# Cross-attention of a Perceiver layer: turning the probabilities by VectorE blocks and a DMA exchange in place of TensorE transposes

## The reference, cut to what matters

```python
x = x + xattn(layernorm(x), ctx, mask, Wq, Wk, Wv, Wo)      # ctx: 32 x 512 x 384
x = x + attn(layernorm(x), wq, wk, wv, wo)
x = x + ffn(layernorm(x), router, W1, b1, W2, b2)
def xattn(x, ctx, mask, ...):                                # 16 heads of 32
    scores = einsum('bhid,bhjd->bhij', q, k) * scale         # 64 queries x 512 keys for each head
    attn = softmax(where(mask, scores, -max), axis=-1)
    return (einsum('bhij,bhjd->bhid', attn, v)).reshape(...) @ Wo
```

## Time and profile before

| what | value |
|---|---|
| median of 3 launches | 1335.34 us (1334.23 to 1335.86) |
| span of the profiled execution | 1332.7 us |
| PE busy | 1313.8 us, 99% of the span |
| DVE, ACT, POOL busy | 52%, 53%, 44% of the span |
| matmul instructions | 13380 |
| mean DMA rate | 50 GB/s |

### The profile page before, as it was taken

How to read it: one execution, slowest core, us unless ns; L and a number is a source line. 1 busy time by engine, 2 the same in 40 slices (tenths; PEclk the granted TensorE clock), 3 DMA queues, 4 the chain that set the end, 5 groups by cost and what they waited for, 6 DMA issues and landing times.

```text
span 1332.7 us, 33915 instructions
## 1 busy us (share of the span) xinstructions
PE 1313.8 (99%) x13380; PEld 1057.2 (79%) x13380; DVE 691.3 (52%) x1693; ACT 710.4 (53%) x1380; POOL 585.8 (44%) x316
## 2 busy tenths in 40 slices
PE   7999999999999999999999999999999998999998
PEld 6877777777777777777777777788998997888786
DVE  4244544545444445545444454456666669755623
ACT  6455656666566656566565666674332345634231
POOL 6722522332243234224323422576666565473562
PEclk9999999999999999999999999999999999999999
DMA  7101010111111111110101113010000001323241
GB/s 262 60 27 35 28 59 26 33 42 42 33 33 51 33 33 42 42 33 26 59 26 33 34 51 128 15 58 2 2 3 3 1 18 49 96 95 96 80 141 63
DMA packets 39316, 66.46 MB, mean 50 GB/s; under 512 B 4177, under 2 KB 8529, under 8 KB 39249
## 3 DMA queue, kind: packets, MB, share of 16 engines
q1 hardware_dynamic: 38816, 64.70, 14.9%
q10 hardware_dynamic: 432, 0.79, 0.2%
HBM read 61.28 MB, written 4.19 MB: 49 GB/s over the span
## 4 chain that ended last, share of the span: by engine, by line
PE 95%; DVE 3%; issue 1%; DMA 1%; SPq 0%; ACT 0%; POOL 0%; POOLq 0%; DVEq 0%
PE psum L205 41%; PE psum L253 8%; PE psum L2031 7%; PE psum L1678 7%; PE psum L1021 6%; PE psum L223 5%; PE psum L241 5%; PE psum L262 3%; PE psum L1010 3%; PE psum L1041 3%; PE psum L777 2%; PE psum L1052 1%; PE psum L1060 1%; PE psum L1070 1%; DMA tok<-in_x 1%
## 5 line engine op out<-in xcount | busy, mean ns | idle before, releaser
L303 ACT ACTIVATE PT<-psum 128x512 f32<-128x512 f32 x256 | 153.2, 598 | 227.1 <-PE psum L253 227.1
L290 ACT ACTIVATE prob<-prob,nmx 128x512 f32<-128x512 f32 x256 | 182.5, 714 | 96.4 <-DVE nmx L351 96.4
L365 DVE COPY V<-psum 128x512 f32<-128x512 f32 x128 | 88.5, 692 | 228.1 <-PE psum L205 228.1
L351 DVE CUSTOM_DVE_ANT_0 prob<-psum,mbias 128x512 f32<-128x512 f32 x256 | 165.4, 684 | 66.1 <-PE psum L223 66.1
L498 POOL TENSOR_SCALAR ctx_a<-ctx_r 128x1536 fp32r<-128x1536 f32 x16 | 65.4, 4088 | 279.2 <-PE psum L205 279.0
L296 ACT ACTIVATE prob<-prob,rinv 128x512 f32<-128x512 f32 x256 | 182.5, 713 | 0.0
L498 POOL TENSOR_SCALAR ctx_b<-ctx_r 128x1536 fp32r<-128x1536 f32 x16 | 65.4, 4088 | 235.5 <-PE psum L205 235.5
L253 PEld LDWEIGHTS psum<-ident,prob 128*128 128x128 f32 x1024 | 127.5, 141 | 32.8
L253 PE MATMUL psum<-ident,prob 128*128 128x128 f32 x1024 | 153.1, 272 | 0.0
L205 PE MATMUL psum<-wv_h,ctx_b 128*128 128x512 f32 x384 | 144.4, 417 | 0.0
L205 PE MATMUL psum<-wv_h,ctx_a 128*128 128x512 f32 x384 | 142.1, 412 | 0.0
(11 more groups left out here) (238 smaller groups left out, 2934.4 us busy)
## 6 DMA issues: line engine op xcount, KB each, us to landing
ctx_r<-in_ctx SPq DMA_DIRECT2D x32, 768.0 KB, 4.6
w_r<-in_L_ffn_W SPq DMA_DIRECT2D x64, 256.0 KB, 2.9
xres<-in_x SPq DMA_DIRECT2D x16, 256.0 KB, 2.6
out<-tok SPq DMA_DIRECT2D x13, 256.0 KB, 3.4
tok<-in_x SPq DMA_DIRECT2D x3, 1024.0 KB, 11.9
mask<-in_mask_BxS_bf SPq DMA_DIRECT2D x32, 64.0 KB, 4.2
tok<-in_x SPq DMA_DIRECT2D x4, 256.0 KB, 3.5
wq_r<-in_L_xattn_Wq SPq DMA_DIRECT2D x4, 256.0 KB, 5.0
```

What stands on the lines that cost most here:

```text
L290: act.activation(prob[:, r, :], prob[:, r, :], ACT.Exp, bias=nmx[:, r:r + 1], scale=-1.0, accum_out=rsum[:, r:r + 1]).then_inc(s_ex, 1)
L303: act.activation(PT[:, r, :, :].rearrange("p k n -> p (k n)"), T_bank, ACT.Copy).then_inc(s_Pt, 1)
L351: dve.tensor_tensor_reduce(prob[:, r, :], S_bank[r], mbias[:, b, :], 1.0, 3.0e38, ALU.add, ALU.min, nmx[:, r:r + 1]).then_inc(s_mx, 1)
L365: dve.tensor_copy(item_place(q, m), KV_bank[m % 2]).then_inc(s_KVe, 1)
```

## The change

In tiles 0 to 14 (60 groups) TensorE no longer transposes probabilities and ScalarE no longer copies `PT`. VectorE turns each scaled slot in 32x32 blocks into `blocks` (`dve_blocks`, one instruction of 128x512 for each slot), which leaves each block in its own 32 partitions. SyncE then exchanges the 4 x 4 grid of 32-partition parts with 16 DMAs of 64 KB each from `blocks` to `turned` (`sp_exchange`). `blocks` and `turned` have two buffers by the parity of q. The value products of a group read `turned` two groups later instead of one. The output product moves from q = 0 to q = 1, between items 1 and 2, into the bank that the transposes used; the residual addition moves to the end of VectorE's list at q = 1, the statistics to the end at q = 2. VectorE still copies all four items; the semaphore of those copies is split in two. Tile 15 keeps the transposes (`pe_last_group` and so on); its q = 0 does the value products of two earlier groups, and the loads of the self-attention weights wait for the last exchange. An unused function `dve_slot` goes.

```diff
+        blocks = [m(f"blocks{i}", [P, 4, 4, KT, HD], F32) for i in range(2)]
+        turned = [Map(nc, pt_at)("turned0", [P, 4, 4, KT, HD], F32), m("turned1", [P, 4, 4, KT, HD], F32)]
...
+        def pe_exchanged_values(pe, g, q, first=False):
+            i, z = GPT * g + q, (q - 2) % GPT
+            pe.wait_ge(s_ex4[z], 256 * (g + 1 if q >= 2 else g))
+            if not (first and q == 2):
+                pe.wait_ge(s_Ol, i - 2)
+            value_products(pe, z, lambda c, kt, r: turned[z % 2][:, 2 * c:2 * c + 2, r, kt, :], PV_bank)
...
-        def pe_group(pe, g, q, first=False, fill=None, filled=None):
+        def pe_group(pe, g, q, first=False):
             pe_scores(pe, g, q, first)
-            if not (first and q == 0):
-                pe_values(pe, g, q, first)
+            if not (first and q < 2):
+                pe_exchanged_values(pe, g, q, first)
+            pe_item(pe, g, q, 0)
+            pe_item(pe, g, q, 1)
+            if q == 1 and not first:
+                pe_outputs(pe, g, T_bank)
+            pe_item(pe, g, q, 2)
+            pe_item(pe, g, q, 3)
...
+        def act_group(act, g, q, first=False):
             act_exp(act, g, q, 0)
             act_exp(act, g, q, 1)
+            if not (first and q < 2):
+                act_outputs(act, g, q, 2, first)
+            act_norm(act, g, q, 0)
+            act_exp(act, g, q, 2)
+            act_norm(act, g, q, 1)
+            act_exp(act, g, q, 3)
+            act_norm(act, g, q, 2)
+            act_norm(act, g, q, 3)
...
+        def dve_blocks(dve, g, q, r, first=False):
+            i = GPT * g + q
+            dve.wait_ge(s_pn, 4 * i + r + 1)
+            if r == 0 and not (first and q < 2):
+                dve.wait_ge(s_PV, i - 1)
+            dve.transpose(blocks[q % 2][:, :, r, :, :].rearrange("p g k n -> p k g n"),
+                          prob[:, r, :].rearrange("p (k g n) -> p k g n", g=4, n=HD)).then_inc(s_bl, 1)
...
+        def dve_group(dve, g, q, first=False):
+            dve_max(dve, g, q, 0, first)
             dve_max(dve, g, q, 1)
             dve_max(dve, g, q, 2)
             dve_inverse(dve, g, q, 0)
             dve_max(dve, g, q, 3)
             dve_inverse(dve, g, q, 1)
+            if not (first and q < 2):
+                dve_outputs(dve, g, q, 2)
+            dve_blocks(dve, g, q, 0, first)
+            dve_item(dve, g, q, 0)
+            dve_inverse(dve, g, q, 2)
+            dve_blocks(dve, g, q, 1)
+            dve_inverse(dve, g, q, 3)
+            dve_item(dve, g, q, 1)
+            dve_blocks(dve, g, q, 2)
+            dve_blocks(dve, g, q, 3)
+            dve_item(dve, g, q, 2)
+            dve_item(dve, g, q, 3)
+            if q == 1 and not first:
+                dve_add(dve, g, T_bank)
+            if q == 2 and not first:
+                dve_stats(dve, g)
...
+        def sp_exchange(sp, g, q, first):
+            i = GPT * g + q
+            sp.wait_ge(s_bl, 4 * i + 4)
+            settle(sp)
+            if not (first and q < 2):
+                sp.wait_ge(s_PV, i - 1)
+            settle(sp)
+            for e in range(4):
+                for f in range(4):
+                    sp.dma_start(turned[q % 2][f * HD:(f + 1) * HD, e].rearrange("p r k n -> p (r k n)"),
+                                 blocks[q % 2][e * HD:(e + 1) * HD, f].rearrange("p r k n -> p (r k n)"))\
+                        .then_inc(s_ex4[q], 16)
...
         def sp_tile(sp, g, first, last):
             if last:
+                sp.wait_ge(s_ex4[3], 256 * (G - 1))
                 for i, r, w in ((1, kw_r, ak), (0, qw_r, aq), (2, vw_r, av)):
                     sp.dma_start(r[:], w.rearrange("(t p) n -> p t n", p=P)).then_inc(s3_w[i], 16)
+                sp_tokens(sp, g, first)
+                return
+            sp_context(sp, g, 2, False)
+            sp_exchange(sp, g, 0, first)
+            sp_exchange(sp, g, 1, first)
+            sp_context(sp, g, 3, False)
+            sp_exchange(sp, g, 2, first)
+            sp_tokens(sp, g, first)
+            sp_exchange(sp, g, 3, first)
...
             pool.wait_ge(s3_w[1], 16)
+            pool.wait_ge(s_PV, OWN)
             pool_split(pool, kw_h, kw_l, kw_r)
```

More of the change, by code:

```diff
@@ L196, in pe_item @@
                     pe.wait_ge(s_cx, 2 * (BPG * g + q // HALVES + 2))
-                if not (isinstance(i, int) and i < 0 and m < 2):
-                    pe.wait_ge(s_KVe, 4 * i + 3 + m)
+                if m >= 2:
+                    pe.wait_ge(s_Ke, 2 * i + 1 + m)
+                elif not (isinstance(i, int) and i < 0):
+                    pe.wait_ge(s_Ve, 2 * i + 1 + m)
             for c in parts:
@@ L208, in pe_item, with pe_scores @@
                 ins.then_inc(s_KV, 1)
-        def pe_scores(pe, g, q, first):
+        def pe_scores(pe, g, q, first, last=False):
             i, b, a = GPT * g + q, q // HALVES, q % HALVES
@@ L214, in pe_scores @@
                 pe.wait_ge(s_qb, BPG * g + b + 1)
-            pe.wait_ge(s_KVe, 4 * i + 2)
+            pe.wait_ge(s_Ke, 2 * i + 2)
             if not (first and q == 0):
                 pe.wait_ge(s_mx, 4 * i)
-            if q == 1 and not first:
+            if q == 1 and last:
                 pe.wait_ge(s_x1, g + 1)
@@ L225, in pe_scores, with value_products @@
             ins.then_inc(s_S, 1)
-        def pe_values(pe, g, q, first, place=PV_bank):
-            i, z = GPT * g + q, (q - 1) % GPT
+        def value_products(pe, z, source, place):
             b, a = z // HALVES, z % HALVES
[L232 to L236, removed]
             for c in range(2):
@@ L258, in pe_outputs @@
             pe.wait_ge(s_Ol, GPT * g)
-            pe.wait_ge(s_mx, 4 * GPT * g + 1 if place is Wo_bank else 4 * GPT * g)
+            if place is Wo_bank:
+                pe.wait_ge(s_mx, 4 * GPT * g + 1)
+            elif place is T_bank:
+                pe.wait_ge(s_x1, g)
+            else:
+                pe.wait_ge(s_mx, 4 * GPT * g)
             for n in range(DT):
@@ L273, in pe_group @@
             pe_item(pe, g, q, 1)
+            if q == 0:
+                pe_exchanged_values(pe, g, 1)
             if filled:
                 pe.wait_ge(*filled)
-            pe_turn(pe, g, q, 0, first)
-            if q == 0 and not first:
-                pe_outputs(pe, g)
+            pe_turn(pe, g, q, 0)
             pe_item(pe, g, q, 2, (0, 1))
             pe_turn(pe, g, q, 1)
+            if q == 0:
+                pe_outputs(pe, g)
             pe_item(pe, g, q, 2, (2,))
@@ L334, in act_group @@
                 act_exp(act, g, q, 3)
-                act_turn(act, g, q, 0, first)
+                act_turn(act, g, q, 0)
             act_norm(act, g, q, 2)
@@ L342, in act_group, with dve_max @@
             act_turn(act, g, q, 3)
-        def dve_max(dve, g, q, r):
+        def dve_max(dve, g, q, r, first=False, last=False):
             i, b = GPT * g + q, q // HALVES
@@ L347, in dve_max @@
                 dve.wait_ge(s_S, i + 1)
+                if not (first and q == 0) and not (last and q > 0):
+                    dve.wait_ge(s_bl, 4 * i)
                 if q % HALVES == 0:
@@ L380, in dve_group, with dve_last_group @@
             dve_inverse(dve, g, q, 1)
-            if not (first and q == 0):
-                dve_outputs(dve, g, q)
+            if not (first and q < 2):
[14 more added lines that the diff above has]
+                dve_stats(dve, g)
+        def dve_last_group(dve, g, q, fill=None):
+            dve_max(dve, g, q, 0, last=True)
+            dve_max(dve, g, q, 1)
+            dve_max(dve, g, q, 2)
+            dve_inverse(dve, g, q, 0)
+            dve_max(dve, g, q, 3)
+            dve_inverse(dve, g, q, 1)
+            dve_outputs(dve, g, q, 2 if q == 0 else 1)
             dve_item(dve, g, q, 0)
@@ L388, in dve_group @@
             dve_inverse(dve, g, q, 3)
-            if q == 0 and not first:
+            if q == 0:
+                dve_outputs(dve, g, 1, 2)
+            dve_item(dve, g, q, 2)
+            if q == 0:
                 dve_add(dve, g)
-            dve_item(dve, g, q, 2)
-            if q == 1 and not first:
+            if q == 1:
                 dve_stats(dve, g)
@@ L420, in layer_norm @@
                            bias=sh3[:, bass.ds(t, 1)], scale=rs3[:, bass.ds(t, 1)]).then_inc(s3_xn, 1)
[L422 to L463, removed]
         def sp_context(sp, g, b, first):
@@ L475, in sp_context, with sp_tokens @@
             sp.dma_start(mask8[:, b % BPG, :], mask[bass.ds(n, 1), :].broadcast_to([P, SK])).then_inc(s_mraw[b % BPG], 16)
[L477 to L482, removed]
+        def sp_exchange(sp, g, q, first):
[10 more added lines that the diff above has]
+                        .then_inc(s_ex4[q], 16)
+        def sp_tokens(sp, g, first):
             if not first:
@@ L486, in sp_tile @@
             sp.dma_start(xres[:], xt[:, bass.ds(g, 1), :]).then_inc(s_xr, 16)
-            if not last:
-                sp_context(sp, g, 3, False)
+        def sp_tile(sp, g, first, last):
```

(25 more changed lines are left out.)

91 lines of the change are left out of this document (56 added, 35 removed).

## The result

The changed kernel takes 1246.45 us (median of 4 launches, 1244.41 to 1247.91) against 1335.17 us before (4 launches); the ratio is 0.9336, 95% interval 0.9323 to 0.9349. That is 88.7 us faster where 104 were forecast. The profiled execution has a span of 1245.9 us, 86.8 less than before. So the direction and most of the size came, and some 15 us did not.

A forecast was written before the change was run, and what follows sets the result against it. TensorE, busy 1313.8 of 1332.7 us, was taken as the bound. Turns 110, less 4 for statistics and 2 for tile 15's stall, gave 104: span 1228.7, plus 2.6 for launches, 1231 us; range 1222 to 1265.

The forecast's parts named there:

- TensorE idle before the value products with a DMA as releaser: Sign of being wrong: TensorE waiting before the value products until an exchange DMA lands; no size given.
- a stall in tile 15 over 5 us: Sign of being wrong: a stall in tile 15 of over 5 us, where the sum allowed 2 us.
- One of its signs of being right: The exchange between `blocks` and `turned` lands within 10 us of its first issue.
- The turns, 110 us: TensorE's list without the four turns: a group falls from 12.31 to 10.49, saving 1.84 in each of 60 groups.
- T = 0.72: VectorE's transpose of one 128x512 slot takes 0.72 us, with 0.43 and 1.21 as the ends.
- Rival B: VectorE is the bound because its transpose takes near 1.21 us: 75 us saved, 1260 us; chance 11%.
- Rival C: VectorE's transpose is held under GpSimd's splits as a cast is: 83 us lost, 1314 us; chance 7%.
- The statistics, 0.3 us a tile: VectorE's statistics, last at q = 2, delay the maxima and item 0's copy of q = 3: 14 x 0.3 = 4 us lost.
- 16 issues a group at 0.38 to 0.43: SyncE's exchange issues take 6.1 to 6.9 us of a 10.49 us group, other loads 0.45, and hide.
- a stall of 2: In tile 15, q = 0 reads the last exchange at 6.4 while it lands at about 8: 2 us lost.
- Rival D: The exchange does not keep pace, so waits for `turned` replace the turns; slower from 0.77 us a DMA; chance 6%.
- The estimate from the Trainium skill: A 64 KB load takes 0.95 us, so an exchange is 15.2 us, longer than the group; kernel ends near 1510.

The follow-up runs named there:

- the split: Against the changed kernel, ScalarE issues 4 of the 16 DMAs of each exchange, 12 stay on SyncE: 1232.38 us, ratio 0.9244.
- the experiment with the statistics alone: Against the changed kernel, VectorE's statistics at q = 2 move ahead of the copy of item 2, nothing else: 1245.39 us, ratio 0.9336.
- the one with both: Against the changed kernel, ScalarE issues 4 of 16 exchange DMAs and the statistics move ahead of item 2's copy: 1223.7 us, ratio 0.9167.
- the one with 8 and 8: As the one with both, but ScalarE issues 8 of the 16 exchange DMAs in place of 4: 1267.85 us.

## Why the prediction was right, and where it was off

The measured 1246.45 lies in the stated range, near the middle, and 15 us above the forecast of 1231. What makes the kernel faster, the turns off TensorE's list, was foreseen; that SyncE's list would keep pace with room was wrong, and that the total stayed in the range all the same is in part luck. Two of the prediction's own signs of being wrong are in the trace: TensorE idle before the value products with a DMA as releaser, and a stall in tile 15 over 5 us (5.28). One of its signs of being right is missing: the exchange lands about 12 us after its first issue, not within 10.

By spans, 17.2 us are missing (1245.9 against 1228.7). Tiles 1 and 2 hold 4.2 of them, tiles 3 to 14 1.8, tile 15 5.0 and the time behind cross-attention 3.5; the rest, under 3, was not followed. By the prediction's steps:

**The turns, 110 us: right.** A group was to take 10.49 and takes 10.43, a saving of 1.88 for 1.84. Turns priced by the chain (0.44 and the restart behind each) carried the whole saving; TensorE's busy time fell by 101.6.

**T = 0.72: right, 0.698.** Rival B (T near 1.21) is out.

**Rival C, the port shared with GpSimd: out.** Timelines of GpSimd and of VectorE in one stretch of the changed kernel:

```profile
515.23 4.09 POOL L570 TENSOR_SCALAR ctx_b<-ctx_r 128x1536 fp32r<-128x1536 f32 x1 [13.80 <-DMA ctx_r<-in_ctx]
```

```profile
511.86 0.68 DVE L492 BATCH_NORM_STATS2 st<-tok 128x6 f32 x1
...
513.39 0.69 DVE L408 CUSTOM_DVE_ANT_0 prob<-psum,mbias 128x512 f32<-128x512 f32 x1 [0.20 <-issue]
...
516.46 0.71 DVE L431 STREAM_TRANSPOSE blocks<-prob 128x512 f32<-128x512 f32 x1 [0.21 <-ACT prob L339]
517.09 0.65 DVE L423 COPY K<-psum 128x512 f32<-128x512 f32 x1
```

The transpose at 516.46 lies wholly under GpSimd's instruction and takes 0.71; over all 240 they take 668 to 715 ns. GpSimd's instruction is not held either: 4.09 us, as before. The transpose is of the statistics' kind, not of the cast's, which adds an instruction to those of which the Trainium skill (SBUF — State Buffer, "Who interferes with whom") says that they do not contend.

**The statistics, 0.3 us a tile: under-sized.** It was 0.54. The same rows show why: the maxima of q = 3 start at 513.39, 2.24 after the scores at 511.15, not 1.4 + 0.7, and the copy of item 0 ends at 517.74, where TensorE wanted it at 517.5 and restarts only behind the semaphore. 14 x 0.24 = 3 us more. It hides behind the turns in the sum: 4 x 0.06 us a tile came out better there, so the forecast's tile, 4 x 10.49 + 2.77 + 0.3 = 45.03, meets the 45.0 of the split by two misses that cancel. And by the experiment with the statistics alone this would not have moved the time while SyncE's list was as long as the tile.

**"16 issues a group at 0.38 to 0.43": the step that failed.** They cost 0.63 from start to start. The sum of 6.1 to 6.9 us of 10.49 was 10.1, and with the context, mask and residual loads the list became as long as the tile. Two things were off in the price. It came from loads out of HBM, and it took the length of an issue (0.43) where the distance to the next (0.48 and 0.47 for the issues at 857.10, 857.58 and 858.05 in the kernel before) fills the list. The other loads were mis-sized too: 0.45 a group counts the issues alone, and with the gaps around them they are 4.7 us a tile, 1.2 a group. From this come three losses, which the split removes but for 1.6 us: tiles 1 and 2 (47.3 and 47.0 for 45.0, 4.2 us; SyncE's pace was 0.66 in tile 0, where 32 issues took 21.11 us), waits of 0.1 to 0.2 us a tile in the loop, and tile 15. There the forecast had the last exchange at 8 us into the tile and a stall of 2; it began 1.8 us late behind SyncE's other work, took 10.11, and landed at about 11.7, a stall of 5.3, with the slow clock behind it, so that q = 0 took 23.08 for the 16.1 that its work needs.

That the kernel lost no more by this step is luck. The list came out at 45.2 us against TensorE's 45.0. An estimate with the 0.68 that the prediction names: 64 x 0.68 + 4.7 = 48.2 us a tile, 15 x 3.2 = 48 us more than the forecast, 1279, outside the range.

**Rival D: right in kind, short in size.** Its threshold, 0.77 us for each DMA, was not reached at 0.63, but the kernel sits much nearer to it than the forecast allowed, and with halved DMAs it is on the far side. The threshold itself leaves out SyncE's other work; with it, it is (52.0 - 4.7) / 64 = 0.74. The value that the prediction set against it, 0.68, was nearer to the truth than the one it took. It was not the dearest issue on record, though. The trace of the kernel before has this one (timeline of SPq):

```profile
889.50 0.76 SPq L1793 DMA_DIRECT2D before<-in_before  x1
```

D's own mechanism, DMAs that run one after another, is not what happens: issued 0.63 apart, they land 2.0 us after their issue, so three are under way at once. The estimate from the Trainium skill (DMA: Bandwidth & Descriptors, "Measured"), 15.2 us for an exchange, did not come true either: 16 issues and the last landing are about 12 us, and the 10.1 of these that matter are SyncE's.

**What stays open.** From the start of the last group of cross-attention to the end the changed kernel takes 449.4 us, before 445.9. 2.5 us of it is one idle stretch of TensorE between 905 and 960 that the trace puts down to "issue", with a granted clock of 0.97 there. The kernels with the split alone and with the statistics alone show no such stretch, the one with both shows 1.8, the one with 8 and 8 shows 1.9 and the kernel before 0.9. It follows no edit of cross-attention; what it comes from stays open. The late weights of self-attention are not enough for it: the split also loads them behind the last exchange and has the shortest time there of the four kernels with four launches, 445.0 us. Nor was it tried why a source in SBUF makes an issue dearer.

## What to carry to other kernels

When a change puts many DMAs into a queue, count the issues times the start-to-start time of issues of the same kind, source memory included, and set the sum against the period of the loop, as one does for an engine. Two resources that are equally long hide each other: freeing one alone (the statistics) showed nothing, and its worth came out only behind the other's. If the issuing engine is the bound, fewer or wider DMAs help, and so does a second engine that has room at that point of its list, but not more than the room.

## What the runs showed of the hardware that was not expected

An issue cost SyncE 0.59 us (0.63 from start to start) when source and destination were both in SBUF, at every size tried: medians of 591 ns for 32 KB and for 64 KB on 32 partitions, 602 ns for 256 KB on 128 partitions. With the source in HBM and all else equal the median is 421 ns (0.46 from start to start). On ScalarE's queue four take 2.45 us, nearly the same price. VectorE's 32x32 block transpose of 128x512 4-byte values takes 698 ns, with its results written in runs of 32 elements, and is not slowed under GpSimd's 128x1536 TENSOR_SCALAR (0.71 at 516.46). After 5.3 us without work TensorE ran at the lower clock level for about 3.4 us: value products took 1.94 us in place of 1.10.
